# A GRU that feeds a ternary-weight FFN: load order, weight casts and step 0's products are rearranged at the start

## The chip, the cores and the metric

The kernel runs on one core of a Trainium2 chip. Its time is the device time of one execution in microseconds (us), as the median of several runs. The profile is of one further execution.

## What is computed

The input is x (128 sequences, 32 time steps, 256 features) with a start state cond (128 x 256). A GRU runs over the 32 steps, one after the other, since each step needs the state of the step before. Its states go through a feed-forward network with ternary weights, and x is added to the result.

```python
def cell(h, x):
    gi = x @ W_ih + b_ih
    gh = h @ W_hh + b_hh
    i_r, i_z, i_n = jnp.split(gi, 3, axis=-1)
    h_r, h_z, h_n = jnp.split(gh, 3, axis=-1)
    r = jax.nn.sigmoid(i_r + h_r)
    z = jax.nn.sigmoid(i_z + h_z)
    n = jnp.tanh(i_n + r * h_n)
    h_new = (1.0 - z) * n + z * h
    return (h_new, h_new)
...
wq_gu = ternary_quant(w_gate_up)          # groups of 64, scale = mean |w|
gate, up = jnp.split(jnp.einsum('bsd,hd->bsh', hs, wq_gu), 2, axis=-1)
h = jax.nn.silu(gate) * up
out = x + jnp.einsum('bsh,dh->bsd', rms_norm(h), ternary_quant(w_proj))
```

W_ih and W_hh are 256 x 768, w_gate_up is 2048 x 256, w_proj 256 x 1024.

## The kernel before, in words

**Layout.** The batch of 128 lies on the partitions. The 256 features are two halves of 128 (KD = 2, index k), so a product x @ W is two accumulating matmuls into PSUM. Every fp32 operand of a product is split into a high part (rounded to the matmul's fp32r type, `_hi`) and a low part (what the rounding left, `_lo`), and a product is three passes: hi x hi, hi x lo, lo x hi (`three_passes`, L672 to L680). So the GRU weights, raw in `wi` and `wh` (tiles of the program's `work` buffer, by which name the trace calls them), become `wi_hi`, `wi_lo`, `wh_hi`, `wh_lo`: ScalarE (ACT) casts the high part (L418, L427), VectorE (DVE) subtracts to get the low part (L586, L592). The state and the input are split in the same way (`xT_hi`, `xT_lo`; the start state goes to `grp_hi`, `grp_lo`).

**One GRU step t.** The bank `ps_rz` (512 columns) holds the sums for r and z, `ps_n` the two sums for n. ACT seeds both with the biases from a copy in SBUF, `bias` (L352 to L359). TensorE (PE) adds the input's products (`input_rz`, `input_n`) and the state's (`state_product`). ACT takes the sigmoid (`rz_gates`, L350), DVE forms r * h_n (`r_hn`, L498) and the sum `n_pre`, ACT the tanh, DVE the new state, PE transposes it, ACT and DVE split it for the next step.

**The order.** The order of each engine's work is written out by hand: each engine has a program of its own, runs it strictly in order, and waits on semaphores where it says so. Steps go in groups of GS = 4. The FFN on group g-1 runs between the GRU's parts of group g. In groups 0 and 1 (steps 0 to 7) the FFN weights are also made ternary, in 12 units of 128 x 512: ACT takes absolute value and sign (`q_abs`, `q_sign`, L396 and L401), PE sums groups of 64 (L795), ACT makes means (L408), GpSimd (POOL) and DVE form the quantized weights. The steady state is a loop over groups 2 to 6; group 7 and a last FFN stand behind it.

**The start, which the change touches.**

- SyncE's queue (SP) issues all loads in one order: both bias rows into `b_row`, the inputs of steps 0 and 1, W_ih in two halves, the transposed start state `cT`, W_hh in two halves, the start state `h_nat`, then the FFN weights and the rest of x (L237 to L251).
- ACT, in order: activation table, `xT_hi` of step 0, two casts of `wi_hi`, the two bias copies from PSUM (L420, L422), the start state's high part (L424), two casts of `wh_hi`, `xT_hi` of step 1, `q_abs` twice, `q_sign` twice. Then follows step 0's sigmoid.
- DVE, in order: sum of the bias rows (L581), `xT_lo` of step 0, two `wi_lo`, the start state's low part, two `wh_lo`, `xT_lo` of step 1. Then follows step 0's `r_hn`.
- PE, in order (L840 to L852): the biases are broadcast over the 128 partitions by matmuls of a row of ones with the bias rows in plain fp32, 256 + 256 columns into `ps_n` and 512 into `ps_rz`; four matmuls on an identity, `keep_clock(4)`; then the wait for both halves of `wi_lo`, step 0's input products, the wait for both halves of `wh_lo`, and step 0's state products.

Of the kernel before, what the change touches and what calls it, by code (L numbers as in the profile page):

```python
# [11 lines left out]
P = 128  # L31
KD = 2
GS = 4
# [3 lines left out]

# [17 lines left out]
def gru_ffn(nc, x, x_t, cond, cond_t, w_ih, w_hh, b_ih, b_hh, w_gate_up_t, w_proj_t, out):  # L57
# [7 lines left out]
    with ExitStack() as ctx:  # L65
# [78 lines left out]

# [7 lines left out]
        b_sum_ok, biased = sem("b_sum_ok"), sem("biased")  # L152
# [37 lines left out]

# [5 lines left out]

# [32 lines left out]
        def _(sp):  # L229
# [7 lines left out]
            for i, b in enumerate((b_ih, b_hh)):  # L237
                sp.dma_start(b_row[:, i, :], b.rearrange("(o n) -> o n", o=1)).then_inc(ld_b, 16)
            sp.dma_start(xT_all[:, :, 0:2, :], xt[:, :, 0:2, :]).then_inc(ld_x0, 16)
            for k in range(KD):  # L240
                sp.dma_start(wi[:, k], w_ih[k * P:(k + 1) * P, :]).then_inc(ld_wi[k], 16)
            sp.dma_start(cT[:], cond_t.rearrange("(k p) b -> p k b", p=P)).then_inc(ld_cT, 16)
            for k in range(KD):
                sp.dma_start(wh[:, k], w_hh[k * P:(k + 1) * P, :]).then_inc(ld_wh[k], 16)
            sp.dma_start(h_nat[:, 1, :], cond).then_inc(ld_c, 16)
# [38 lines left out]

# [62 lines left out]
        def _(act):  # L347
# [4 lines left out]
            def seed_rz(t):  # L352

                act.wait_ge(rz_ok, t)
                nc.scalar.copy(ps_rz[:], bias[:, 0, :]).then_inc(rz_seed, 1)
# [55 lines left out]

            act.wait_ge(consts, 2)
# [3 lines left out]
            for k in range(KD):  # L416
                act.wait_ge(ld_wi[k], 16)
                nc.scalar.copy(wi_hi[:, k], wi[:, k]).then_inc(wi_hi_ok, 1)  # L418
            act.wait_ge(biased, 1)
            nc.scalar.copy(bias[:, 1, :], ps_n[:]).then_inc(n_seed, 1)  # L420
            act.wait_ge(biased, 2)
            nc.scalar.copy(bias[:, 0, :], ps_rz[:]).then_inc(rz_seed, 1)  # L422
            act.wait_ge(ld_cT, 16)
            nc.scalar.copy(state("hi", GS - 1), cT[:]).then_inc(h_hi, 1)  # L424
            for k in range(KD):
                act.wait_ge(ld_wh[k], 16)
                nc.scalar.copy(wh_hi[:, k], wh[:, k]).then_inc(wh_hi_ok, 1)  # L427
            input_hi(1, 1)
# [65 lines left out]
        def _(dve):  # L494
# [88 lines left out]
            input_lo(0, 0)  # L583
# [87 lines left out]
        def _(pe):  # L671
# [10 lines left out]
            def input_rz(t, b):  # L682
                pe.wait_ge(rz_seed, t + 1)
                if isinstance(t, int) and 2 <= t < 2 + GS:
                    pe.wait_ge(x_lo_early, t - 1)
                else:
                    pe.wait_ge(x_lo, t + 1 if isinstance(t, int) and t < 2 else t + 1 - GS)
                three_passes(ps_rz[:], xT_hi[:, b], xT_lo[:, b], wi_hi, wi_lo, slice(0, 512), False)

            def input_n(t, b):  # L690
                pe.wait_ge(n_seed, t + 1)
                three_passes(ps_n[:, 0:D], xT_hi[:, b], xT_lo[:, b], wi_hi, wi_lo, slice(512, G3), False)

            def state_product(t, s):
# [11 lines left out]
                three_passes(ps_n[:, D:2 * D], hi, lo, wh_hi, wh_lo, slice(512, G3), True).then_inc(n_sum, 1)  # L706

# [105 lines left out]
            def iteration(g, ffn, carry):  # L813
                for s in range(GS):
                    t = GS * g + s
                    last = isinstance(g, int) and g == NG - 1
                    state_product(t, s)
# [21 lines left out]

            pe.wait_ge(consts, 6)  # L840
            pe.wait_ge(ld_b, 32)
            for i in range(2):
                mm = pe.matmul(ps_n[:, i * D:(i + 1) * D], ones_row[:], b_row[:, i, 2 * D:G3],
                               start=(i == 0), stop=(i == 1), skip_group_check=True)
# [47 lines left out]
```

## Time and profile before

| | before |
|---|---|
| median of 3 runs | 377.59 us (377.42 to 377.64) |
| profiled execution: span, first to last instruction | 376.7 us |
| what lies around the span, against the median of the runs | 0.9 us |
| busy: PE | 350.5 us (93%) |
| busy: DVE | 258.6 us (69%) |
| busy: ACT | 221.4 us (59%) |
| busy: POOL | 199.3 us (53%) |
| mean granted TensorE clock | 0.978 |

No device time of the profiled execution itself is given beside its span, so the 0.9 us compares that span with the median of the other runs. Busy shares average over the whole span; the start, the stretch with the quantization, and the loop have different limits and are read apart.

### The profile page before, as it was taken

To read this page: it belongs to the slowest core of one execution; us is meant where nothing else is said; L and a number is where in the kernel's file an instruction comes from. 1 tells how busy PE (TensorE), PEld (TensorE's weight loads), DVE (VectorE), ACT (ScalarE), POOL (GpSimd) and SP (SyncE) were. 2 spreads that over 40 slices of the span, in tenths; PEclk is the share of its full clock that TensorE was granted. 3 is DMA by queue.
4 is the path that set the end of the run, shared out by engine and by line. 5 is a ranking of instruction groups with operands and counts; after the bars stand their busy time and mean duration, and the time that the engine had idled before them with its cause. 6 is when DMAs were issued, how large, how long until landed. Compare 5 with 4: busy or idle time off the path is not lost.

```text
span 376.7 us, 5881 instructions
## 1 busy us (share of the span) xinstructions
PE 350.5 (93%) x1959; PEld 300.8 (80%) x1962; DVE 258.6 (69%) x484; ACT 221.4 (59%) x434; POOL 199.3 (53%) x165
## 2 busy tenths in 40 slices
PE   6957787788999999999999999999999999999995
PEld 3745566567888889888988888888988898888885
DVE  3499999997586566856585558656685658556644
ACT  5755576554746655666745574665566674547650
POOL 1067765585555536444625555553644472557882
PEclk9998888999999999999999999999999999999998
DMA  7980000370001000100010000100010001000101
GB/s 241 375 359 2 2 0 0 113 334 1 3 3 54 1 2 0 56 0 0 0 56 0 0 0 3 53 0 0 0 56 0 0 0 58 0 0 2 56 2 56
DMA packets 5394, 17.75 MB, mean 47 GB/s; under 512 B 386, under 2 KB 2050, under 8 KB 4996
## 3 DMA queue, kind: packets, MB, share of 16 engines
q1 hardware_dynamic: 5380, 17.57, 12.1%
q8 instruction: 8, 0.13, 0.2%
q14 instruction: 6, 0.05, 0.0%
HBM read 13.38 MB, written 4.19 MB: 47 GB/s over the span
## 4 chain that ended last, share of the span: by engine, by line
PE 75%; DVE 15%; issue 6%; DMA 1%; ACT 1%; SPq 0%; POOL 0%; DVEq 0%; POOLq 0%
PE ps_out L757 15%; PE ps_gate L718 14%; PE ps_up L718 13%; PE ps_rz L699 3%; PE ps_rz L700 3%; PE ps_rz L703 3%; PE ps_n L675 3%; PE ps_rz L675 3%; PE ps_n L676 3%; PE ps_n L678 3%; PE ps_rz L676 3%; PE ps_rz L678 3%; DVE q_sk L571 2%; DVE wguT L578 2%; PE ps_hT L711 2%
## 5 line engine op out<-in xcount | busy, mean ns | idle before, releaser
L311 POOL TENSOR_TENSOR hid_lo<-work,hid_hi 128x512 fp32r<-128x512 f32 x63 | 83.9, 1333 | 123.0 <-ACT hid_hi L378 123.0
L318 POOL TENSOR_TENSOR sq_sum<-sq_sum,work 128x512 f32<-128x512 f32 x54 | 70.8, 1310 | 0.0
L524 DVE TENSOR_TENSOR work<-work,ps_gate 128x512 f32<-128x512 f32 x64 | 43.8, 685 | 38.9 <-ACT work L374 38.1
L718 PE MATMUL ps_up<-grp_hi,wguT 128*128 128x512 f32 x118 | 47.4, 402 | 5.3 <-DVE work L534 5.3
L718 PE MATMUL ps_gate<-grp_hi,wguT 128*128 128x512 f32 x128 | 51.4, 401 | 0.0
L718 PE MATMUL ps_gate<-grp_lo,wguT 128*128 128x512 f32 x128 | 50.8, 397 | 0.0
L378 ACT CAST hid_hi<-work 128x512 fp32r<-128x512 f32 x63 | 38.8, 616 | 19.2 <-DVE work L534 19.2
L350 ACT ACTIVATE rz<-ps_rz 128x512 f32<-128x512 f32 x32 | 19.1, 596 | 50.8 <-PE ps_rz L703 50.8
L498 DVE TENSOR_TENSOR r_hn<-rz,ps_n 128x256 f32<-128x256 f32 x32 | 13.4, 419 | 48.7 <-PE ps_n L678 48.7
L534 DVE TENSOR_TENSOR work<-work,ps_up 128x512 f32<-128x512 f32 x59 | 40.5, 687 | 8.7 <-PE ps_up L718 7.2
L718 PE MATMUL ps_up<-grp_lo,wguT 128*128 128x512 f32 x118 | 46.4, 393 | 0.0
L374 ACT ACTIVATE work<-ps_gate 128x512 f32<-128x512 f32 x64 | 37.7, 589 | 11.0 <-PE ps_gate L718 11.0
L757 PEld LDWEIGHTS ps_out<-wpT,hid_hi 128*128 128x128 f32 x256 | 37.9, 189 | 4.3 <-DVE o_st L548 0.5
L757 PE MATMUL ps_out<-wpT,hid_hi 128*128 128x256 f32 x256 | 41.1, 283 | 0.1
L757 PE MATMUL ps_out<-wpT,hid_lo 128*128 128x256 f32 x256 | 41.0, 282 | 0.0
L757 PEld LDWEIGHTS ps_out<-wpT,hid_lo 128*128 128x128 f32 x256 | 35.1, 189 | 0.0
L388 ACT ACTIVATE work<-work 128x512 f32<-128x512 f32 x55 | 34.6, 629 | 0.0
L718 PEld LDWEIGHTS ps_up<-grp_hi,wguT 128*128 128x128 f32 x118 | 22.4, 189 | 11.4 <-DVE work L534 7.0
L294 POOL TENSOR_TENSOR o_st<-q_scale,q_abs 128x512 bf16<-128x512 bf16 x12 | 19.3, 1612 | 15.4 <-DVE q_scale L559 15.4
L675 PE MATMUL ps_rz<-wi_hi,xT_hi 128*128 128x512 f32 x64 | 26.2, 409 | 1.3 <-DVE wi_lo L586 0.8
L718 PEld LDWEIGHTS ps_gate<-grp_hi,wguT 128*128 128x128 f32 x128 | 24.4, 191 | 3.6
L718 PEld LDWEIGHTS ps_gate<-grp_lo,wguT 128*128 128x128 f32 x128 | 24.3, 190 | 3.4
(115 smaller groups left out, 772.1 us busy)
## 6 DMA issues: line engine op xcount, KB each, us to landing
x_all<-in_x_dram SPq DMA_DIRECT2D x1, 4096.0 KB, 12.2
out_dram<-o_st SPq DMA_DIRECT2D x7, 512.0 KB, 2.7
xT_all<-in_x_dram SPq DMA_DIRECT2D x1, 3072.0 KB, 19.5
x_all<-in_L_ffn_w_gate_up_dram SPq DMA_DIRECT2D x4, 512.0 KB, 9.2
x_all<-in_L_ffn_w_proj_dram SPq DMA_DIRECT2D x1, 1024.0 KB, 12.7
work<-in_L_cond_W_ih_dram SPq DMA_DIRECT2D x2, 384.0 KB, 4.2
work<-in_L_cond_W_hh_dram SPq DMA_DIRECT2D x2, 384.0 KB, 5.9
xT_all<-in_x_dram SPq DMA_DIRECT2D x1, 768.0 KB, 8.4
```

Source lines behind the costliest of these rows:

```text
L311: nc.gpsimd.tensor_tensor(hid_lo[:, j % RING], hid[:, j % 2], f32(hid_hi[:, j % RING]), ALU.subtract).then_inc(hid_lo_ok, 1)
L318: nc.gpsimd.tensor_tensor(sq_sum[:], sq_sum[:], hid_sq[:, j % 2], ALU.add).then_inc(sq_added, 1)
L374: nc.scalar.activation(sg[:, j % 2], ps_gate[:, j % 2], ACT.Sigmoid).then_inc(sg_ok, 1)
L378: nc.scalar.copy(hid_hi[:, j % RING], hid[:, j % 2]).then_inc(hid_hi_ok, 1)
L388: nc.scalar.activation(hid_sq[:, j % 2], hid[:, j % 2], ACT.Square).then_inc(hid_sq_ok, 1)
L524: nc.vector.tensor_tensor(gsg[:, j % 2], sg[:, j % 2], ps_gate[:, j % 2], ALU.mult).then_inc(gsg_ok, 1)
L534: nc.vector.tensor_tensor(hid[:, j % 2], gsg[:, j % 2], up_bank(G, j)[:], ALU.mult).then_inc(hid_ok, 1)
L675: pe.matmul(dst, hi[:, k, :], w_hi[:, k, cols], start=False, stop=False, skip_group_check=True)
L676: pe.matmul(dst, hi[:, k, :], w_lo[:, k, cols], start=False, stop=False, skip_group_check=True)
L678: mm = pe.matmul(dst, lo[:, k, :], w_hi[:, k, cols], start=False, stop=stop and k == KD - 1, skip_group_check=True)
L718: mm = pe.matmul(bank, w, part[:, k].rearrange("p s b -> p (s b)"), start=(k == 0 and i == 0), stop=(k == KD - 1 and i == 1))
L757: mm = pe.matmul(ps_out[:, s, :], part[:, j % RING, s * P:(s + 1) * P], wpT[:, j, :], start=(j == 0 and s % 2 == 0 and part is hid_hi), st ...
```

## The change

- SP's queue issues W_ih's two halves first, then W_hh's, then the FFN weights and x as before. The two bias rows, the inputs of steps 0 and 1, `cT` and `h_nat` are issued from ACT's program, ahead of its table load.
- DVE, not ACT, casts `wi_hi`; `xT_lo` of step 0 is put between the two casts.
- Step 0's input products are ordered by pass and by half k: hi x hi as each `wi_hi` comes, then lo x hi, then hi x lo as each `wi_lo` comes. Step 0's state products are ordered likewise (`first_input`, `first_state_product`).
- The biases for `ps_rz` and `ps_n` are no longer copied to SBUF before step 0's products are added to them. Instead PE makes the same bias sums once more, in the two banks of `ps_gate`, behind step 0's input products. ACT copies `bias` from there, behind its `wh_hi` casts.
- Nothing changes behind step 0, but for the semaphore counts of the seeds.

```diff
 # SyncE
-            for i, b in enumerate((b_ih, b_hh)):
-                sp.dma_start(b_row[:, i, :], b.rearrange("(o n) -> o n", o=1)).then_inc(ld_b, 16)
-            sp.dma_start(xT_all[:, :, 0:2, :], xt[:, :, 0:2, :]).then_inc(ld_x0, 16)
             for k in range(KD):
                 sp.dma_start(wi[:, k], w_ih[k * P:(k + 1) * P, :]).then_inc(ld_wi[k], 16)
-            sp.dma_start(cT[:], cond_t.rearrange("(k p) b -> p k b", p=P)).then_inc(ld_cT, 16)
             for k in range(KD):
                 sp.dma_start(wh[:, k], w_hh[k * P:(k + 1) * P, :]).then_inc(ld_wh[k], 16)
-            sp.dma_start(h_nat[:, 1, :], cond).then_inc(ld_c, 16)
 # ScalarE
+            for i, b in enumerate((b_ih, b_hh)):
+                act.dma_start(b_row[:, i, :], b.rearrange("(o n) -> o n", o=1)).then_inc(ld_b, 16)
+            act.dma_start(xT_all[:, :, 0:2, :],
+                          x_t.rearrange("(k p) t b -> p k t b", p=P)[:, :, 0:2, :]).then_inc(ld_x0, 16)
+            act.dma_start(cT[:], cond_t.rearrange("(k p) b -> p k b", p=P)).then_inc(ld_cT, 16)
+            act.dma_start(h_nat[:, 1, :], cond).then_inc(ld_c, 16)
             act.wait_ge(consts, 2)
             nc.scalar.activation(table[:], ones[:], ACT.Sigmoid)
             act.wait_ge(ld_x0, 16)
             input_hi(0, 0)
-            for k in range(KD):
-                act.wait_ge(ld_wi[k], 16)
-                nc.scalar.copy(wi_hi[:, k], wi[:, k]).then_inc(wi_hi_ok, 1)
-            act.wait_ge(biased, 1)
-            nc.scalar.copy(bias[:, 1, :], ps_n[:]).then_inc(n_seed, 1)
-            act.wait_ge(biased, 2)
-            nc.scalar.copy(bias[:, 0, :], ps_rz[:]).then_inc(rz_seed, 1)
             act.wait_ge(ld_cT, 16)
             nc.scalar.copy(state("hi", GS - 1), cT[:]).then_inc(h_hi, 1)
             for k in range(KD):
                 act.wait_ge(ld_wh[k], 16)
                 nc.scalar.copy(wh_hi[:, k], wh[:, k]).then_inc(wh_hi_ok, 1)
+            act.wait_ge(biased, 1)
+            for i in range(2):
+                nc.scalar.copy(bias[:, i, :], ps_gate[:, i, :]).then_inc(bias_ok, 1)
             input_hi(1, 1)
 # VectorE
-            input_lo(0, 0)
+            for k in range(KD):
+                dve.wait_ge(ld_wi[k], 16)
+                nc.vector.tensor_copy(wi_hi[:, k], wi[:, k]).then_inc(wi_hi_ok, 1)
+                if k == 0:
+                    input_lo(0, 0)
 # TensorE: step 0's state product
+            def first_state_product():
+                targets = ((ps_rz[:], slice(0, 512)), (ps_n[:, D:2 * D], slice(512, G3)))
+                hi, lo = state("hi", GS - 1), state("lo", GS - 1)
+                def product(part, w, k, dst, cols, stop=False):
+                    return pe.matmul(dst, part[:, k, :], w[:, k, cols], start=False, stop=stop,
+                                     skip_group_check=True)
+                pe.wait_ge(h_hi, 1)
+                for k in range(KD):
+                    pe.wait_ge(wh_hi_ok, k + 1)
+                    for dst, cols in targets:
+                        product(hi, wh_hi, k, dst, cols)
+                pe.wait_ge(h_lo, 1)
+                for k in range(KD):
+                    for dst, cols in targets:
+                        product(lo, wh_hi, k, dst, cols)
+                for (dst, cols), full in zip(targets, (rz_sum, n_sum)):
+                    for k in range(KD):
+                        pe.wait_ge(wh_ok, k + 1)
+                        mm = product(hi, wh_lo, k, dst, cols, k == KD - 1)
+                    mm.then_inc(full, 1)
 # TensorE: the start
-            for i in range(2):
-                mm = pe.matmul(ps_n[:, i * D:(i + 1) * D], ones_row[:], b_row[:, i, 2 * D:G3],
-                               start=(i == 0), stop=(i == 1), skip_group_check=True)
-            mm.then_inc(biased, 1)
-            pe.wait_ge(b_sum_ok, 1)
-            pe.matmul(ps_rz[:], ones_row[:], b_row[:, 0, 0:2 * D], start=True, stop=True).then_inc(biased, 1)
+            def biases(rz_bank, n_bank):
+                for i in range(2):
+                    pe.matmul(n_bank[:, i * D:(i + 1) * D], ones_row[:], b_row[:, i, 2 * D:G3],
+                              start=(i == 0), stop=(i == 1), skip_group_check=True)
+                pe.wait_ge(b_sum_ok, 1)
+                return pe.matmul(rz_bank, ones_row[:], b_row[:, 0, 0:2 * D], start=True, stop=True)
+            def first_input():
+                targets = ((ps_rz[:], slice(0, 512)), (ps_n[:, 0:D], slice(512, G3)))
+                def product(part, w, k):
+                    for dst, cols in targets:
+                        pe.matmul(dst, part[:, 0, k, :], w[:, k, cols], start=False, stop=False,
+                                  skip_group_check=True)
+                pe.wait_ge(x_hi, 1)
+                for k in range(KD):
+                    pe.wait_ge(wi_hi_ok, k + 1)
+                    product(xT_hi, wi_hi, k)
+                pe.wait_ge(x_lo, 1)
+                for k in range(KD):
+                    product(xT_lo, wi_hi, k)
+                for k in range(KD):
+                    pe.wait_ge(wi_ok, k + 1)
+                    product(xT_hi, wi_lo, k)
+            biases(ps_rz[:], ps_n[:])
             keep_clock(4)
-            pe.wait_ge(wi_ok, KD)
-            input_rz(0, 0)
-            input_n(0, 0)
-            pe.wait_ge(wh_ok, KD)
+            first_input()
+            biases(ps_gate[:, 0, :], ps_gate[:, 1, :]).then_inc(biased, 1)
             iteration(0, False, False)
```

Two places show how the rows of an engine's program move. First PE, between `keep_clock` and step 0's state product; `ps_gate` is the bank that the FFN's gate uses later. Before:

```order
L675 MATMUL ps_n<-wi_hi,xT_hi 128x256
L676 MATMUL ps_n<-wi_lo,xT_hi 128x256
L678 MATMUL ps_n<-wi_hi,xT_lo 128x256 x2
L699 MATMUL ps_rz<-wh_hi,grp_hi 128x512
L700 MATMUL ps_rz<-wh_lo,grp_hi 128x512
```

The end of the input products and the begin of the state products, in the program of the change:

```order
L858 MATMUL ps_rz<-wi_lo,xT_hi 128x512
L858 MATMUL ps_n<-wi_lo,xT_hi 128x256
L847 MATMUL ps_gate<-b_row,ones_row 128x256 x2
L850 MATMUL ps_gate<-b_row,ones_row 128x512
L691 MATMUL ps_rz<-wh_hi,grp_hi 128x512
L691 MATMUL ps_n<-wh_hi,grp_hi 128x256
```

The bias matmuls, which before stood only ahead of `keep_clock`, now stand a second time between the two products. The second place is ACT's program from the table load to step 0's sigmoid, before:

```order
L413 ACT_TABLE_LOAD
L413 ACTIVATE table<-ones 128x1
L370 CAST xT_hi<-xT_all 128x256
L418 CAST wi_hi<-work 128x768 x2
L420 COPY bias<-ps_n 128x512
L422 COPY bias<-ps_rz 128x512
L424 CAST grp_hi<-cT 128x2x128
L427 CAST wh_hi<-work 128x768 x2
```

And with the change, down to the sigmoid, its last row:

```order
L390 ACT_TABLE_LOAD
L390 ACTIVATE table<-ones 128x1
L341 CAST xT_hi<-xT_all 128x256
L394 CAST grp_hi<-cT 128x2x128
L397 CAST wh_hi<-work 128x768 x2
L400 COPY bias<-ps_gate 128x512 x2
L341 CAST xT_hi<-xT_all 128x256
L367 ACTIVATE q_abs<-x_all 128x512 x2
L372 ACTIVATE q_sign<-x_all 128x512 x2
L319 ACTIVATE rz<-ps_rz 128x512
```

The bias copies moved from ahead of the start state's cast to behind the `wh_hi` casts. Five instructions (the second `xT_hi`, two `q_abs`, two `q_sign`) stand between them and the sigmoid.

## Rows read from the trace of the kernel before

**Rows 1.** Windows: busy time of the engines, granted clock, DMA share, in three stretches

```profile
0.00:16.60 16.60, 13.05 (x40) 9.67 (x40) 5.61 (x8) 9.47 (x17) 1.40 (x12) 1.00 0.86 302
16.60:88.90 72.30, 54.12 (x247) 41.67 (x248) 70.50 (x110) 42.55 (x88) 47.61 (x35) 0.91 0.29 116
88.90:376.70 287.80, 283.30 (x1674) 249.47 (x1674) 182.47 (x367) 169.35 (x331) 150.27 (x118) 0.99 0.04 15
```

**Rows 2.** Chain that ended last: start us, length us, what; start and hand-over

```profile
2.38 4.99 DMA work<-in_L_cond_W_ih_dram
...
7.40 0.84 ACT wi_hi L418
...
9.30 0.77 PE ps_rz L675
...
15.19 0.60 PE ps_rz L703 x2
...
16.64 0.43 DVE r_hn L498
...
88.92 1.19 PE ps_up L718 x4
```

**Rows 3.** Timeline of PE: start us, us, instruction, tiles, count, idle before

```profile
2.79 2.04 PE L843 MATMUL ps_n<-b_row,ones_row 1*128 1x256 f32 x4 [2.79 <-DMA b_row<-in_L_cond_b_hh_dram]
4.62 1.91 PE L847 MATMUL ps_rz<-b_row,ones_row 1*128 1x512 f32 x2
6.46 2.08 PE L836 MATMUL ps_hT<-ident 128*128 128x128 f32 x8
```

**Rows 4.** Timeline of PE: input products cold, and step 1's warm

```profile
10.29 0.63 PE L675 MATMUL ps_rz<-wi_hi,xT_hi 128*128 128x512 f32 x1
...
10.72 0.63 PE L676 MATMUL ps_rz<-wi_lo,xT_hi 128*128 128x512 f32 x1
...
23.86 0.40 PE L676 MATMUL ps_rz<-wi_lo,xT_hi 128*128 128x512 f32 x1
...
24.10 0.40 PE L675 MATMUL ps_rz<-wi_hi,xT_hi 128*128 128x512 f32 x1
```

**Rows 5.** Timeline of ACT up to step 0's sigmoid (L350)

```profile
8.14 0.58 ACT L420 COPY bias<-ps_n 128x512 f32<-128x512 f32 x1
8.62 0.59 ACT L422 COPY bias<-ps_rz 128x512 f32<-128x512 f32 x1
9.09 0.42 ACT L424 CAST grp_hi<-cT 128x256 fp32r<-128x256 f32 x1
...
10.86 0.41 ACT L370 CAST xT_hi<-xT_all 128x256 fp32r<-128x256 f32 x1
12.02 1.15 ACT L396 ACTIVATE q_abs<-x_all 128x512 bf16<-128x512 f32 x2 [0.74 <-DMA x_all<-in_L_ffn_w_gate_up_dram]
13.07 1.13 ACT L401 ACTIVATE q_sign<-x_all 128x512 bf16<-128x512 f32 x2
15.83 0.60 ACT L350 ACTIVATE rz<-ps_rz 128x512 f32<-128x512 f32 x1 [1.62 <-PE ps_rz L703]
```

**Rows 6.** Windows, PE alone: busy, granted clock, DMA share, GB/s, around a rise

```profile
28.30:29.00 0.70, 0.69 (x6) 1.00 0.00 0
29.00:32.40 3.40, 3.40 (x11) 0.50 0.02 5
32.40:33.00 0.60, 0.60 (x7) 0.98 0.00 0
```

**Rows 7.** Timeline of DVE: the split of W_hh's two halves

```profile
10.27 1.83 DVE L592 TENSOR_TENSOR wh_lo<-work,wh_hi 128x768 fp32r<-128x768 f32 x2 [0.31 <-ACT wh_hi L427]
```

**Rows 8.** One line of DVE: ns min/median/max, a cast of 768 columns

```profile
L627 DVE CAST grp_lo<-new_lo x8: 551/551/1190, 49.9 to 342.8; 128x768 fp32r<-128x768 f32 x8
```

**Rows 9.** Timeline of SP's queue: issues of bias row and first input

```profile
1.14 0.23 SPq L238 DMA_DIRECT2D b_row<-in_L_cond_b_hh_dram  x1
...
1.42 0.42 SPq L239 DMA_DIRECT2D xT_all<-in_x_dram  x1
```

More of the change, by code:

```diff
@@ L151, in gru_ffn @@
         wi_hi_ok, wi_ok, wh_hi_ok, wh_ok = sem("wi_hi_ok"), sem("wi_ok"), sem("wh_hi_ok"), sem("wh_ok")
-        b_sum_ok, biased = sem("b_sum_ok"), sem("biased")
+        b_sum_ok, biased, bias_ok = sem("b_sum_ok"), sem("biased"), sem("bias_ok")
         q_sum = sem("q_sum")
@@ L354, in seed_rz @@
                 act.wait_ge(rz_ok, t)
+                if isinstance(t, int) and t == 1:
+                    act.wait_ge(bias_ok, 2)
                 nc.scalar.copy(ps_rz[:], bias[:, 0, :]).then_inc(rz_seed, 1)
@@ L682, in input_rz @@
             def input_rz(t, b):
-                pe.wait_ge(rz_seed, t + 1)
+                pe.wait_ge(rz_seed, t)
                 if isinstance(t, int) and 2 <= t < 2 + GS:
@@ L686, in input_rz @@
                 else:
-                    pe.wait_ge(x_lo, t + 1 if isinstance(t, int) and t < 2 else t + 1 - GS)
+                    pe.wait_ge(x_lo, 2 if isinstance(t, int) and t == 1 else t + 1 - GS)
                 three_passes(ps_rz[:], xT_hi[:, b], xT_lo[:, b], wi_hi, wi_lo, slice(0, 512), False)
             def input_n(t, b):
-                pe.wait_ge(n_seed, t + 1)
+                pe.wait_ge(n_seed, t)
                 three_passes(ps_n[:, 0:D], xT_hi[:, b], xT_lo[:, b], wi_hi, wi_lo, slice(512, G3), False)
@@ L816, in iteration @@
                     last = isinstance(g, int) and g == NG - 1
-                    state_product(t, s)
+                    if isinstance(g, int) and t == 0:
+                        first_state_product()
+                    else:
+                        state_product(t, s)
                     for u in summed(g, s):
```

## The prediction, made before the result was known

> **What bounds the kernel now.** I read the windows first, to see which engine is full in which stretch. In [rows 1] the first 16.6 us have no full engine; from 16.6 to 88.9 DVE works 70.5 of 72.3 us; from 88.9 on PE works 283.3 of 287.8 us. The chain of waits [rows 2] says the same: a load of W_ih until 7.4, its split, PE's products from 9.30, and from step 0's `r_hn` at 16.64 a chain of DVE instructions until PE takes over at 88.92. Between 16.64 and 88.92 the chain holds over 150 pieces and no DMA. The change touches nothing behind step 0, so all depends on one number: when `r_hn` of step 0 starts. I take every microsecond won or lost there as handed on to the end.
>
> **What is won: the wait for W_ih.** The loads of both halves of W_ih lose one 256 KB load and two bias rows ahead of them, and are issued some 1.1 us earlier. The second half landed at 7.4 [rows 2]; now it lands between 6.2 and 7.4. DVE casts instead of ACT: nearest rows are DVE's cast of the same size, 0.55 us at best [rows 8], and its subtraction, about 0.95 us each [rows 7]. At the worst `wi_hi` is ready at 7.4 + 0.95 = 8.4 and the second `wi_lo` at 8.4 + 1.9 = 10.3; at the best 8.7. Before, PE began at 9.30. Now PE's row has `keep_clock` until 6.46 + 2.08 = 8.5 [rows 3], so the input products start at 8.5, not earlier, whatever the loads do: 0.8 us won. They don't wait again: hi x hi and lo x hi take 4 x (0.43 + 0.21) = 2.6 us at the slow pace, so the last `wi_lo` is wanted at 11.7 and is there at 10.3. For the same reason the order by passes wins nothing more; the halves are all ready in time. The W_hh side has slack too: at worst `wh_lo` is ready at 10.3 + 0.4 + 1.9 = 12.6 and is wanted last of all.
>
> The granted DMA share is already 0.86 over the first 16.6 us [rows 1]. The Trainium skill (DMA: Bandwidth & Descriptors, Rules for kernel authors) says that spreading DMAs over two issuing engines does not help bandwidth and saves only issue time. By that rule the second queue gives only the later end of 6.2 to 7.4, and the trace's share agrees; the sum is the same at either end, since PE starts at 8.5.
>
> **What is paid on PE: the biases a second time.** The bias matmuls stand again between input and state products. The first set took from 2.79 to 6.46, 3.67 us [rows 3], at the slow pace. Which pace? A 512-column matmul took 0.43 us from start to start at 10.3 and 0.24 at 23.9 [rows 4], so PE was at 1.2 GHz and then at 2.4, though the clock column reads 1.00 in both. The input products are six of 512 and six of 256 columns: 6 x 0.43 + 6 x 0.21 = 3.84 us slow. If the clock rises at r, what is left runs in half the time, and input and second biases end at T = (r + 8.5 + 3.84 + 3.67) / 2 = (r + 16.0) / 2.
>
> When does it rise? Before, PE worked unbroken from 9.30 and was at the fast pace only at about 15.4 (the last pair of `ps_rz` took 0.60 instead of 0.86, [rows 2]), 6.1 us later. At 28.30 it resumed, and the granted clock was 0.50 until 32.4 and 0.98 after, 4.1 us after work resumed [rows 6]. Now there is no break between `keep_clock` and products: counted 4.1 us from the start of `keep_clock` (6.46) the rise is at 10.6, from the products' start (8.5) at 12.6, and with 6.1 us at 14.6. I take 12.0, near the products' case, because the biases and `keep_clock` ran from 2.79 to 8.5 and the clock had not risen by 9.3. T = 14.0. Ends: a rise at 8.5 gives T = 12.3, none gives 16.0.
>
> The Trainium skill (TensorE: Matmul & The Clock Gate, Part 1) says that the clock is throttled by default and that activity is looked at in free-running windows that don't restart with a kernel, so the point of the rise moves. By it T could lie anywhere between the ends above; the two delays here, 4.1 and 6.1 us, agree that it is not fixed.
>
> The bias rows come by ACT's queue now. Before, the second was issued at 1.14 and PE started at 2.79; the 256 KB load issued at 1.42 took until 4.45. So the biases start between 0 and 1.4 us later [rows 9, 3]. I take 0, since these are 3 KB rows, ahead in their queue. ACT's five issues cost it about 2 us, 0.23 to 0.43 each [rows 9], ahead of its table load; the load of x lands no earlier anyway, and ACT is idle later, so nothing.
>
> **What is paid on ACT: a queue behind the biases.** This decides. ACT runs in order, and the bias copies now wait for T. Behind them stand `xT_hi` of step 1, two `q_abs`, two `q_sign`, and only then step 0's sigmoid. Costs from [rows 5], start to start: the two copies 9.09 - 8.14 = 0.95; `xT_hi` 0.40; `q_abs` 13.07 - 12.02 = 1.05; `q_sign` 1.13. Together 3.5 us. Before, ACT had done all of it by 14.2 and sat idle 1.62 us until PE was ready at 15.83. Now the sigmoid starts at T + 3.5; with its 0.60 and 0.1 for the hand-over `r_hn` starts at T + 4.2. PE is not the later one: its state products take 3.84 us slow, 2.1 fast, and `rz_sum` comes before the last 0.4 us of them, so T + 3.4 at worst. The casts saved on ACT (2 x 0.83) are saved where ACT would now be idle: nothing. The q loads had landed by 12.02, before they are wanted.
>
> **The sum.** `r_hn` at 14.0 + 4.2 = 18.2 instead of 16.64: 1.6 us later. The profiled span of 376.7 becomes 378.3; the median of the runs is 0.9 us above that span, so 377.6 + 1.6 = **379.2 us**. Behind `r_hn` the order is unchanged and DVE has 1.8 idle us in 72 to take anything up.
>
> **Rivals.** About 0.2%, 0.76 us, is what a measurement can tell from no change.
> 1. *The clock stays down through the second biases.* A rise 6.1 us after 8.5 gives T = 15.3, none 16.0: `r_hn` at 19.5 to 20.2, loss 2.9 to 3.6, about 380.8. For it: the 6.1 us of before, and that the first biases, one row on the contracting side, did not raise the clock. Against it: the dense products now follow work without a gap.
> 2. *The clock rises at once*, at about 8.5 to 10.2. T = 12.3 to 13.1, `r_hn` at 16.5 to 17.3, time 377.5 to 378.3: no change that can be told. For it: the gap of 0.8 us ahead of the products is closed. Against it: 5.7 us of PE work before 8.5 raised nothing. A delay that is taken up between 16.6 and 88.9 would look the same.
> 3. *Faster: the start of PE itself is at the fast pace.* If the clock were up by about 6, `keep_clock` ends at 7.3 and the products wait only for the splits: the last `wi_lo` at 8.7 to 10.3 plus 0.35, biases 1.84, T = 11.0 to 12.4, `r_hn` at 15.2 to 16.6. The middle is 0.8 to 1.0 us earlier: 376.7. It decides for faster once T is under 16.64 - 0.76 - 4.2 = 11.7. Against it: the slow pace at 10.3.
> 4. *The overlap is empty*: the reordered passes do not do what they say, since all halves are ready at 8.5. That is part of the forecast; only with W_ih later than 9 would they count.
>
> **How the numbers follow.** The forecast's case (T from 13.3 to 14.8, so 378.5 to 380.0) gets 0.60, rival 1 0.18, rival 2 0.16, rival 3 0.06. The range takes in the forecast's case, rival 1 but for its extreme, and the upper part of rival 2: 378.0 to 381.0. Slower 0.78, same 0.16, faster 0.06.
>
> **What would show it.** In the profile after: the input products start at about 8.5 with no idle time before them; `ps_gate` matmuls of the biases follow at 12, ending at 14; ACT's copies of `bias` wait on PE, and its sigmoid L319 starts about 3.5 us behind them with no idle time before it, while PE had finished its state products; `r_hn` at about 18.2 waits for ACT, not PE; PE takes over at about 90.5 instead of 88.9. I am wrong if ACT idles before that sigmoid, if the copies come before 11.7, or if `r_hn` is late and the hand-over to PE at 88.9 is not.

## The result and the profile after

| | before | changed |
|---|---|---|
| median | 377.5 us (377.17 to 377.64, 4 runs) | 381.05 us (380.56 to 381.45, 4 runs) |
| ratio | | 1.0085, 95% interval 1.0067 to 1.0103 |
| profiled span | 376.7 us | 379.0 us |
| granted clock, mean | 0.978 | 0.973 |

The kernel became slower by 0.85%; between the medians lie 3.55 us. (The ratio is taken over the single runs; the two medians divided give 1.0094, inside the interval.) The forecast was 379.2 us (378.0 to 381.0) with 0.78 for slower. The sign is right; the median lies 0.05 us beyond the upper end of the range, and the loss is more than twice the 1.6 us that was forecast.

First the windows of the changed kernel, cut 2.3 us later than those of [rows 1], since the span grew by 2.3 us (us; busy of PE, PEld, DVE, ACT, POOL with counts; granted clock; DMA share; GB/s):

```profile
0.00:18.90 18.90, 13.24 (x47) 9.03 (x47) 6.95 (x12) 8.44 (x16) 1.39 (x12) 1.00 0.94 324
18.90:91.20 72.30, 53.33 (x249) 42.01 (x253) 70.53 (x110) 42.84 (x88) 48.05 (x36) 0.91 0.25 101
91.20:379.00 287.80, 283.48 (x1672) 249.70 (x1670) 181.49 (x365) 168.29 (x330) 149.94 (x118) 0.99 0.04 15
```

So moved, the two long stretches are as in [rows 1]: DVE works 70.5 of 72.3 us, PE 283.5 of 287.8. The start grew. Its chain of waits (start us, us, what):

```profile
17.09 0.52 ACT q_sign L372
17.61 0.49 ACT rz L319
...
18.19 0.43 DVE r_hn L471
...
90.28 1.19 PE ps_up L719 x4
```

Before, this chain came to `r_hn` at 16.64 by way of PE's products [rows 2]. Now it comes by ACT's `q_sign`, and `r_hn` starts at 18.19. PE takes over at 90.28 instead of 88.92. ACT's timeline shows why (start us, us, instruction, idle before it):

```profile
14.15 1.08 ACT L400 COPY bias<-ps_gate 128x512 f32<-128x512 f32 x2 [2.92 <-PE ps_gate L850]
...
15.11 0.42 ACT L341 CAST xT_hi<-xT_all 128x256 fp32r<-128x256 f32 x1
...
15.41 1.16 ACT L367 ACTIVATE q_abs<-x_all 128x512 bf16<-128x512 f32 x2
...
16.47 1.15 ACT L372 ACTIVATE q_sign<-x_all 128x512 bf16<-128x512 f32 x2
...
17.50 0.59 ACT L319 ACTIVATE rz<-ps_rz 128x512 f32<-128x512 f32 x1
```

The bias copies waited 2.92 us for PE, five instructions stood behind them, and the sigmoid began 3.35 us after the start of the copies, with no idle time ahead of it. In [rows 5] the same `q_abs` and `q_sign` were done by 14.2. PE's own timeline, the same columns:

```profile
3.86 2.04 PE L847 MATMUL ps_n<-b_row,ones_row 1*128 1x256 f32 x4 [3.86 <-DMA b_row<-in_L_cond_b_hh_dram]
...
7.54 2.08 PE L840 MATMUL ps_hT<-ident 128*128 128x128 f32 x8
...
9.27 0.77 PE L858 MATMUL ps_rz<-wi_hi,xT_hi 128*128 128x512 f32 x1
...
10.05 0.63 PE L858 MATMUL ps_rz<-wi_hi,xT_hi 128*128 128x512 f32 x1
...
10.99 0.40 PE L858 MATMUL ps_rz<-wi_hi,xT_lo 128*128 128x512 f32 x1
...
12.13 1.13 PE L847 MATMUL ps_gate<-b_row,ones_row 1*128 1x256 f32 x4
...
13.10 1.02 PE L850 MATMUL ps_gate<-b_row,ones_row 1*128 1x512 f32 x2
...
14.04 0.50 PE L691 MATMUL ps_rz<-wh_hi,grp_hi 128*128 128x512 f32 x1
...
15.19 0.40 PE L691 MATMUL ps_rz<-wh_hi,grp_lo 128*128 128x512 f32 x1
```

PE starts 1.07 us later than in [rows 3], for it waits for the bias row; the products start at 9.27, and 512-column matmuls pass from 0.63 to 0.40 us at about 10.6. The second biases end at 14.1. The state products behind them run at the fast pace here, with 0.40 us for 512 columns, and PE is done well before ACT.

Two more things differ. The first inputs land late. These are the issues and the wait:

```profile
1.28 0.22 ACTq L384 DMA_DIRECT2D b_row<-in_L_cond_b_hh_dram  x1
...
1.53 0.42 ACTq L385 DMA_DIRECT2D xT_all<-in_x_dram  x1
...
7.69 0.41 ACT L341 CAST xT_hi<-xT_all 128x256 fp32r<-128x256 f32 x1 [3.17 <-DMA xT_all<-in_x_dram]
...
8.48 0.55 DVE L558 CAST wi_hi<-work 128x768 fp32r<-128x768 f32 x1
8.94 1.82 DVE L563 TENSOR_TENSOR wi_lo<-work,wi_hi 128x768 fp32r<-128x768 f32 x2
```

The 256 KB of x landed 6.1 us after their issue, not 3.0, and DVE's second cast of W_ih stood behind `xT_lo`, which needs them. The last `wi_lo` was ready at 10.8, yet PE did not wait for it: it began at 9.27, straight behind `keep_clock`, with the passes that need `wi_hi` alone. And the last products of the kernel ran at half pace, here in the timeline and in a window of PE alone (busy, granted clock, DMA share, GB/s):

```profile
372.80 1.20 PE L758 MATMUL ps_out<-wpT,hid_hi 128*128 128x256 f32 x4
373.80 1.05 PE L758 MATMUL ps_out<-wpT,hid_lo 128*128 128x256 f32 x4
```

```profile
372.60:374.80 2.20, 2.20 (x10) 0.50 0.00 0
```

In the profile of before, the same last rows run at a granted clock of 1.00:

```profile
371.07 0.72 PE L757 MATMUL ps_out<-wpT,hid_hi 128*128 128x256 f32 x4
371.63 0.63 PE L757 MATMUL ps_out<-wpT,hid_lo 128*128 128x256 f32 x4
```

This is some 0.8 us that the start did not cause directly.

### The profile page after: what moved, and what is told of

Read it like the earlier page. It is cut to its first block, busy times and chain, and to the rows that moved or that the text cites. A ratio compares the mean times of both kernels' runs of the same rounds, so it can differ in the third digit from the quotient of the medians.

```text
span 379.0 us, 5888 instructions
## 1 busy us (share of the span) xinstructions
PE 350.1 (92%) x1965; PEld 300.7 (79%) x1968; DVE 259.0 (68%) x486; ACT 219.6 (58%) x432; POOL 199.4 (53%) x165
## 4 chain that ended last, share of the span: by engine, by line
PE 75%; DVE 15%; issue 5%; DVEq 0%; ACT 0%
PE ps_out L758 16%; PE ps_gate L719 14%; PE ps_up L719 13%; PE ps_rz L676 3%; PE ps_rz L680 3%; PE ps_rz L677 3%; PE ps_n L652 3%; PE ps_n L653 3%; PE ps_n L655 3%; PE ps_rz L653 3%; PE ps_rz L652 3%; PE ps_rz L655 3%; DVE q_sk L544 3%; DVE wguT L551 2%; PE ps_hT L712 2%
## 5 line engine op out<-in xcount | busy, mean ns | idle before, releaser
L345 ACT ACTIVATE work<-ps_gate 128x512 f32<-128x512 f32 x64 | 37.6, 588 | 12.1 <-PE ps_gate L719 12.1
L652 PE MATMUL ps_rz<-wi_hi,xT_hi 128*128 128x512 f32 x62 | 24.8, 400 | 2.0 <-ACT ps_rz L326 2.0
```

Of the source, the lines that this page charges most:

```text
L345: nc.scalar.activation(sg[:, j % 2], ps_gate[:, j % 2], ACT.Sigmoid).then_inc(sg_ok, 1)
L652: pe.matmul(dst, hi[:, k, :], w_hi[:, k, cols], start=False, stop=False, skip_group_check=True)
```

## The experiments

The theory is that of the forecast, the **queue theory**: the bias copies on ACT wait for PE's second biases, and the five instructions behind them hold up step 0's sigmoid. Its rivals: PE's products set it (**PE theory**, in a later form with the clock: **clock theory**), or the late loads do (**load theory**). Every ratio is to runs of the kernel before on the same chip. Kernels 1 to 4 ran on one chip, 5 to 8 on a second, 9 to 11 on a third, 12 on a fourth; medians of different groups are set side by side below, and the medians of the kernel before in these groups are 377.54, 377.46, 377.73 and 377.75 us.

**1. The copies out of the way.**

```diff
-            act.wait_ge(biased, 1)
-            for i in range(2):
-                nc.scalar.copy(bias[:, i, :], ps_gate[:, i, :]).then_inc(bias_ok, 1)
             input_hi(1, 1)
             q_abs_of(0)
             q_abs_of(1)
             q_signs(0)
             q_signs(1)
+            act.wait_ge(biased, 1)
+            for i in range(2):
+                nc.scalar.copy(bias[:, i, :], ps_gate[:, i, :]).then_inc(bias_ok, 1)
```

> The changed kernel, with ACT's two bias copies moved behind the two q_abs and two q_sign, so that only the copies wait for PE's second biases. Queue theory (the five ACT instructions behind the bias wait set step 0's sigmoid): ACT does them while it waited, the sigmoid starts with rz_sum at about 16.0 instead of 17.5, r_hn at about 16.8 instead of 18.19, and the time falls by 1.4 us against the change. PE theory (the second biases and the products behind them set it): r_hn stays at 18.2 and the time stays. Load theory (the late bias rows and first input set it): stays too.

Measured 380.93 us (378.69 to 381.39, 10 runs), ratio to before 1.0077 (1.0055 to 1.0098): no gain on the change. The queue theory missed. Its windows (columns as in the first fence) and timeline:

```profile
10.90:14.30 3.40, 3.40 (x15) 2.18 (x14) 1.49 (x3) 2.50 (x6) 0.00 (x0) 1.00 1.04 407
14.30:17.70 3.40, 3.40 (x11) 2.85 (x11) 0.00 (x0) 1.07 (x2) 0.00 (x0) 0.54 1.08 369
```

```profile
13.42 1.02 PE L850 MATMUL ps_gate<-b_row,ones_row 1*128 1x512 f32 x2
...
16.31 0.63 PE L691 MATMUL ps_rz<-wh_hi,grp_lo 128*128 128x512 f32 x1
...
18.04 0.60 ACT L319 ACTIVATE rz<-ps_rz 128x512 f32<-128x512 f32 x1 [2.50 <-PE ps_rz L691]
```

ACT idles 2.50 us now and PE is the late one. The granted clock fell to 0.54, the 1.2 GHz level, right behind the second biases, though PE had worked without a pause; the state products, down to the sum that the sigmoid needs, took 3.6 us instead of 2.1, and `r_hn` starts at 18.73. Eight of the ten runs lie from 380.5 to 381.4. Two were at 378.7 and 378.8, below even the 379.6 that was expected.

**2 to 4. The second biases and the loads, each undone, and both.** Without the second biases:

```diff
 # ScalarE, behind input_hi(0, 0)
+            act.wait_ge(biased, 1)
+            nc.scalar.copy(bias[:, 1, :], ps_n[:]).then_inc(bias_ok, 1)
+            nc.scalar.copy(bias[:, 0, :], ps_rz[:]).then_inc(bias_ok, 1)
...
-            act.wait_ge(biased, 1)
-            for i in range(2):
-                nc.scalar.copy(bias[:, i, :], ps_gate[:, i, :]).then_inc(bias_ok, 1)
 # TensorE
-            biases(ps_rz[:], ps_n[:])
+            biases(ps_rz[:], ps_n[:]).then_inc(biased, 1)
             keep_clock(4)
+            pe.wait_ge(bias_ok, 2)
             first_input()
-            biases(ps_gate[:, 0, :], ps_gate[:, 1, :]).then_inc(biased, 1)
```

> The changed kernel without PE's second biases: ACT copies the biases out of ps_n and ps_rz behind the first xT_hi, as before the change, and PE waits for the copies before step 0's products. Queue theory: nothing on ACT waits for a late PE result, q_abs starts as soon as its load is there (about 12 to 12.6), r_hn at about 15.5, 2.7 us earlier than the change and 1.1 earlier than before. Load theory: the products still start at 9.3 as the bias rows come late; r_hn no earlier than before, 16.6. If only the 1.8 us of PE work counts, r_hn at 16.4.

With the loads of before:

```diff
 # SyncE
+            for i, b in enumerate((b_ih, b_hh)):
+                sp.dma_start(b_row[:, i, :], b.rearrange("(o n) -> o n", o=1)).then_inc(ld_b, 16)
+            sp.dma_start(xT_all[:, :, 0:2, :], xt[:, :, 0:2, :]).then_inc(ld_x0, 16)
             for k in range(KD):
                 sp.dma_start(wi[:, k], w_ih[k * P:(k + 1) * P, :]).then_inc(ld_wi[k], 16)
+            sp.dma_start(cT[:], cond_t.rearrange("(k p) b -> p k b", p=P)).then_inc(ld_cT, 16)
             for k in range(KD):
                 sp.dma_start(wh[:, k], w_hh[k * P:(k + 1) * P, :]).then_inc(ld_wh[k], 16)
+            sp.dma_start(h_nat[:, 1, :], cond).then_inc(ld_c, 16)
 # ScalarE
-            for i, b in enumerate((b_ih, b_hh)):
-                act.dma_start(b_row[:, i, :], b.rearrange("(o n) -> o n", o=1)).then_inc(ld_b, 16)
...
-            act.dma_start(h_nat[:, 1, :], cond).then_inc(ld_c, 16)
```

> The changed kernel with all loads on SP's queue in the order of before, all else as changed. Bias rows land at 2.8 instead of 3.9, so PE's start, the second biases and the queue behind them all come 1.1 us earlier: r_hn at about 17.1 if the clock rises as early, and the time falls by about 1 us. If the load order of the change is worth anything, the first products wait for wi_hi and r_hn does not move. A late clock rise would hide up to 1.5 us of it.

And with both edits together:

> Loads as before and no second biases; what is left of the change is DVE's cast of W_ih and the products by pass. PE's products start at about 8.5 without a gap, the queue on ACT is free of PE: q_abs at 12.0 when its load lands, sigmoid at 14.3, r_hn at about 15.0, 1.6 us earlier than before: 375.9 us, faster than both kernels. If the q loads landing at 12.0 do not bound it but PE does with a late clock rise, r_hn at 16 and 377. Clock theory of the tail: any run can be 0.8 us longer where the clock falls in the last products, whatever the start does.

| median us | with second biases | without |
|---|---|---|
| loads of the change | 381.05 (the change) | 377.97 (377.14 to 379.43) |
| loads of before | 379.98 (379.56 to 380.16) | 376.73 (376.38 to 377.42) |

The ratios to before are 1.0018 (1.0001 to 1.0035) for the second kernel, 1.0056 (1.0036 to 1.0077) for the third, 0.9976 (0.9962 to 0.999) for the fourth. The second biases cost 3.1 us with the one set of loads and 3.25 with the other; the load order costs 1.1 and 1.2. From the ratios instead of the medians it is 2.5 and 3.0 us, and 1.1 and 1.6. Both are harmful alone and they add up. In the profile of the second kernel `r_hn` is at 15.21, near the 15.5 of the queue theory; that its products still start late, at 9.15, is the share of the loads. From the timeline of the fourth kernel:

```profile
8.06 0.77 PE L857 MATMUL ps_rz<-wi_hi,xT_hi 128*128 128x512 f32 x1
...
14.09 0.60 ACT L324 ACTIVATE rz<-ps_rz 128x512 f32<-128x512 f32 x1
...
14.78 0.42 DVE L470 TENSOR_TENSOR r_hn<-rz,ps_n 128x256 f32<-128x256 f32 x1 [2.71 <-ACT rz L324]
```

PE starts its products straight behind `keep_clock`, and `r_hn` is at 14.78; 15.0 was expected. The gain expected, 1.6 us, was counted from 16.64 and came out as 0.8 (see 8). For the third kernel about 380 was expected, with `r_hn` at 17.1. The time came as expected, `r_hn` did not: in the third kernel the profile fell on a late clock rise: the products start 1.2 us earlier than with the loads of the change, but `r_hn` did not move.

```profile
8.09 0.77 PE L857 MATMUL ps_rz<-wi_hi,xT_hi 128*128 128x512 f32 x1
...
11.44 0.63 PE L857 MATMUL ps_rz<-wi_lo,xT_hi 128*128 128x512 f32 x1
...
18.29 0.42 DVE L470 TENSOR_TENSOR r_hn<-rz,ps_n 128x256 f32<-128x256 f32 x1 [2.21 <-ACT rz L324]
```

The last input products still take 0.63 here, 0.40 in the profile of the change. Seven runs, not one profile, carry the 1.1 us; the slowest of them, 380.16, lies below the fastest of the change, 380.56. Here too the clock fell behind the second biases, at about 15.7, while PE was busy.

**5 and 6. One row or 128.** The second biases contract over one row, that is, only one of the 128 partitions holds values for them. Here they contract over all 128, a matrix of ones with the bias row and 127 rows of zeros, once on the change and once on kernel 1:

```diff
+            nc.gpsimd.memset(b_wide, 0.0).then_inc(wide_ok, 1)
+            pool.wait_ge(wide_ok, 1)
+            nc.gpsimd.memset(ones_wide, 1.0).then_inc(wide_ok, 1)
 # VectorE, behind the sum of the bias rows
+            nc.vector.tensor_copy(b_wide[0:1], b_row[:]).then_inc(wide_row, 1)
 # TensorE, in place of the second biases()
+            pe.wait_ge(wide_ok, 2)
+            pe.wait_ge(wide_row, 1)
+            for i in range(2):
+                pe.matmul(ps_gate[:, 1, i * D:(i + 1) * D], ones_wide, b_wide[:, i, 2 * D:G3],
+                          start=(i == 0), stop=(i == 1), skip_group_check=True)
+            pe.matmul(ps_gate[:, 0, :], ones_wide, b_wide[:, 0, 0:2 * D],
+                      start=True, stop=True).then_inc(biased, 1)
```

`b_wide` is 128 x 1536, `ones_wide` 128 x 128.

> The changed kernel, whose second bias matmuls contract over all 128 rows (a matrix of ones with the bias row and 127 rows of zeros) instead of one; columns and results are the same. Clock theory (the granted clock falls behind the one-row matmuls, and step 0's state products then run at 1.2 GHz): the clock stays at 2.4 GHz through the state products; ACT's queue still sets r_hn at 18.2, so the time falls only by what the slow products had added in the median, to about 380. If the rows make no difference to the clock, no change from 381.0.

> e1_copies_late with the 128-row second biases. Clock theory: neither ACT's queue nor slow products stand in the way; the sigmoid starts at about 16.1, r_hn at 16.8, all runs near the two lowest of e1 (378.7), 2.2 us under e1's median of 380.9. Queue theory alone (clock no part of it): as e1, 380.9. It tells why moving the copies alone gave nothing.

The fifth measured 380.97 (380.52 to 381.26), as the change; its fall of 1 us was not seen. In its profile the clock rises late, at about 12.8, the state products run at 0.40 us for 512 columns, and the sigmoid still waits for ACT's queue, until 18.38. The sixth measured 379.42 (378.76 to 380.86), ratio to before 1.0056 (1.0037 to 1.0075), 1.5 us under kernel 1, with seven of nine runs between 378.8 and 379.7. None of the changed kernel's eight runs (four in the result, four in 12) is under 380.5. The interval of the ratio does overlap that of kernel 1, 1.0055 to 1.0098, whose runs also fall in two groups; it is the count of runs in the lower group, seven of nine against two of ten, that tells them apart. Its timeline:

```profile
13.95 1.02 PE L891 MATMUL ps_gate<-x_all 128*128 128x512 f32 x2
...
15.86 0.39 PE L702 MATMUL ps_rz<-wh_hi,grp_lo 128*128 128x512 f32 x1
...
17.55 0.42 DVE L479 TENSOR_TENSOR r_hn<-rz,ps_n 128x256 f32<-128x256 f32 x1 [5.00 <-ACT rz L327]
```

Behind full-row biases the state products run at 0.39 us. `r_hn` comes 0.75 us later than the 16.8 expected, since the clock rose at about 12.6 and the biases ended at 15.0. So two hindrances stand side by side behind T, the end of the second biases: ACT's queue (3.35 us) and the slowed state products (3.6 us in kernel 1). Taking away one (kernel 1 or kernel 5) gains nothing, since the other takes its place; taking away both (kernel 6) gains 1.5 us. The second hindrance is not in every execution: in the change's first profile the state products took 2.1 us. The expectation of kernel 5 overlooked that slow products can still end within ACT's queue, as they do in kernel 12.

**7. The cast alone.** The kernel before with DVE casting `wi_hi`, `xT_lo` between the two casts, nothing else.

```diff
 # VectorE
-            input_lo(0, 0)
+            for k in range(KD):
+                dve.wait_ge(ld_wi[k], 16)
+                nc.vector.tensor_copy(wi_hi[:, k], wi[:, k]).then_inc(wi_hi_ok, 1)
+                if k == 0:
+                    input_lo(0, 0)
```

> The kernel before, with DVE casting W_ih instead of ACT, nothing else. ACT is then free for the bias copies by 7.5; wi_lo comes 0.1 to 0.3 us earlier than before, as the second half lands at 7.1 to 7.4 and 0.55 + 1.8 us follow. If the cast is what e4 gained by, 376.7; if the products by pass are (they let PE start at 8.1 instead of 9.3), 377.3 or no change.

Measured 378.08 (377.49 to 379.23, 12 runs), ratio 1.0024 (1.001 to 1.0037): slightly slower, which neither theory had. DVE and PE:

```profile
7.08 0.56 DVE L582 CAST wi_hi<-work 128x768 fp32r<-128x768 f32 x1 [0.91 <-DMA work<-in_L_cond_W_ih_dram]
7.56 1.82 DVE L587 TENSOR_TENSOR wi_lo<-work,wi_hi 128x768 fp32r<-128x768 f32 x2
```

```profile
9.43 0.80 PE L676 MATMUL ps_rz<-wi_hi,xT_hi 128*128 128x512 f32 x1 [1.11 <-DVE wi_lo L587]
```

The cast is shorter (0.56 for 0.83), but both subtractions now stand behind the second cast on one engine, where the first used to run while the second half was still on its way. The last `wi_lo` comes at 9.4, no earlier. Why the median is 0.6 us up is open; `r_hn` is at 15.57 in this profile, but the profiled execution, 377.5 us, is one of the two fastest of the twelve.

**8. Before, once more**, without an edit.

> The kernel before, once more, for a second profile of it. If the profile shown of before caught a late clock rise (its span of 376.7 lies 1.0 above the 375.7 that most executions have), this one rises earlier, at about 12 to 13, with r_hn at about 15.5; if not, r_hn is at 16.6 again and the difference lies elsewhere.

377.49 us, span 375.7. PE and DVE:

```profile
12.39 0.34 PE L675 MATMUL ps_n<-wi_hi,xT_hi 128*128 128x256 f32 x1
```

```profile
15.56 0.42 DVE L498 TENSOR_TENSOR r_hn<-rz,ps_n 128x256 f32<-128x256 f32 x1 [2.74 <-PE ps_n L678]
```

The clock rose at 12.4, not 15.4, and `r_hn` is at 15.56. Of the 28 runs beside kernels 1 to 4, the spans lie from 374.2 to 377.1 with the median at 375.7. The profile that the forecast was made on was therefore a late one, by 1.0 us, and what lies around the span is 1.8 us, not 0.9.

**9. The order by passes alone.** Kernel 4 with the casts of W_ih back on ACT:

```diff
 # ScalarE, ahead of the bias copies
+            for k in range(KD):
+                act.wait_ge(ld_wi[k], 16)
+                nc.scalar.copy(wi_hi[:, k], wi[:, k]).then_inc(wi_hi_ok, 1)
 # VectorE
-            for k in range(KD):
-                dve.wait_ge(ld_wi[k], 16)
-                nc.vector.tensor_copy(wi_hi[:, k], wi[:, k]).then_inc(wi_hi_ok, 1)
-                if k == 0:
-                    input_lo(0, 0)
+            input_lo(0, 0)
```

> The kernel before with step 0's products by pass and nothing else changed (ACT casts W_ih, loads on SP, no second biases). The bias copies then end at 9.1 on ACT and PE's products wait for them, so PE starts at 9.1 to 9.3 instead of 9.3 to 9.7 and no pass is ahead of its half: no change from before, 377.4. If the order by passes alone is what e4 gained by, 376.7.

377.94 (376.74 to 378.52), ratio 0.9999 (0.9983 to 1.0016): no change. PE waited for ACT's bias copies until 8.8. Cast and order pay only together: kernels 7 and 9 gain nothing, kernel 4 has both and gains 0.8 us. The profiles suggest why: with the cast on DVE but the old order, PE waits for the last `wi_lo` until 9.43; with the new order but the cast on ACT, it waits for ACT's copies until 8.8; with both it begins at 8.06.

**10 and 11. Better than both.** First `q_sign` behind the sigmoid:

```diff
             q_abs_of(1)
-            q_signs(0)
-            q_signs(1)
 # in step 0, behind q_abs_of(2) and q_abs_of(3)
+                    if isinstance(g, int) and g == 0 and s == 0:
+                        q_signs(0)
+                        q_signs(1)
```

> e4_both_back with the two q_sign moved from ahead of step 0's sigmoid to behind step 1's q_abs. In e4's profile the sigmoid started at 14.09 with q_sign ending there and rz_sum at 14.05, so both set it: if ACT's queue is the later one in most executions, up to 0.8 us less than e4 (376.7), 376.0; if PE is, no change.

376.30 (375.87 to 376.77, 12 runs), ratio 0.9957 (0.9943 to 0.997). The sigmoid starts at 12.97 there:

```profile
12.97 0.60 ACT L324 ACTIVATE rz<-ps_rz 128x512 f32<-128x512 f32 x1
13.66 0.42 DVE L471 TENSOR_TENSOR r_hn<-rz,ps_n 128x256 f32<-128x256 f32 x1 [1.72 <-ACT rz L324]
```

This version is faster than both kernels, by 1.4 us against the one before. Then, on top, full-row work on PE from the start, with the first biases made as in kernel 5 and `keep_clock(4)` cut to one:

```diff
 # TensorE, in place of the waits for consts and ld_b
+            pe.wait_ge(wide_ok, 1)
+            for _ in range(6):
+                pe.matmul(ps_hT[:, 0, :], ones_wide, ones_wide, start=True, stop=True)
+            pe.wait_ge(wide_ok, 2)
+            pe.wait_ge(wide_row, 1)
 # in biases()
-                    pe.matmul(n_bank[:, i * D:(i + 1) * D], ones_row[:], b_row[:, i, 2 * D:G3],
+                    pe.matmul(n_bank[:, i * D:(i + 1) * D], ones_wide, b_wide[:, i, 2 * D:G3],
...
-            keep_clock(4)
+            keep_clock(1)
```

> e9 with PE kept busy from 1.1 us on: six matmuls on a matrix of ones until the bias row is there, then the first biases with 128 rows. Clock theory: with full-row work from the start the clock rises by 8, the input products take 1.9 us instead of 3.8, and only the load of the FFN weights (11.9) and two q_abs hold the sigmoid: r_hn at about 13.8, 375.6. If rows make no difference to the clock, the rise stays at 10.6 to 12.4 and the time is e9's or 0.3 worse, since the bias sums end 1.5 us later.

375.63 (374.8 to 378.17, 12 runs), ratio 0.9944 (0.9925 to 0.9962). The median is lower, but the interval overlaps that of kernel 10, and two of twelve runs are at 378. The profile fell on one of these:

```profile
9.44 0.80 PE L871 MATMUL ps_rz<-wi_hi,xT_hi 128*128 128x512 f32 x1 [0.74 <-ACT bias L402]
...
12.81 0.62 PE L871 MATMUL ps_rz<-wi_lo,xT_hi 128*128 128x512 f32 x1
...
16.16 0.42 DVE L479 TENSOR_TENSOR r_hn<-rz,ps_n 128x256 f32<-128x256 f32 x1 [3.54 <-ACT rz L332]
```

Here full-row work from 1.0 us on, with gaps of 0.6 us ahead of the biases and 0.7 us ahead of the input products, had not raised the clock by 12.8, so the expectation did not hold in this execution. The products also start 1.3 us later than in kernel 10 (9.44 for 8.18), behind ACT's bias copies. Whether the clock rose early in the other executions is not shown.

**12. The change, once more**, without an edit.

> The changed kernel once more, for a second profile of it and more times. Theory: r_hn is at T + 4.1, with T (end of the second biases) between 14.0 and 15.0 by when the clock rises, and the last down product either at 2.4 GHz or, as in the first profile, at 1.2 (0.8 us more). If both vary from execution to execution, this one has a span of 287.8 + 72.1 + r_hn, 0.8 more if the tail is slow; if the slow tail belongs to the change itself, it is slow again.

380.84 (380.57 to 381.35), span 378.8. PE alone in a window, then DVE:

```profile
15.00:18.00 3.00, 3.00 (x12) 0.60 1.09 357
```

```profile
18.89 0.42 DVE L471 TENSOR_TENSOR r_hn<-rz,ps_n 128x256 f32<-128x256 f32 x1 [2.21 <-ACT rz L319]
```

The clock rose 1.5 us later than in the first profile, `r_hn` came 0.7 later, and the last products ran at full pace (0.72 and 0.63 us). `r_hn` and the span are what was expected for an execution with a fast tail. So the slow tail is no fixed part of the change; it is also in the profiles of kernels 1, 9 and 10 and in part in that of kernel 2, and in neither of the two of before. The granted clock fell to a mean of 0.60 in the state products here, from 15.6 on, and `r_hn` still waited for ACT.

## Why the prediction was right, and where it was not

**All hangs on `r_hn` of step 0: right.** From `r_hn` to PE's taking over it is 72.3 us before, 72.1 after, 72.3 in the second profile of before, and 72.1 to 72.2 in kernels 1 to 4. From there to the end it is 287.8, or up to 0.9 more where the last products are slow.

**ACT's queue: right, and not alone.** The sum had T + 4.2; it was 14.1 + 4.1 = 18.2, forecast 18.2. Kernels 1, 5 and 6 show that the state products, at the lower clock behind the one-row biases, would have held `r_hn` up as long wherever the clock falls there: `r_hn` at T + 4.3 in kernel 1. The forecast had 3.4 us for them at worst against 3.5 on ACT, so the tie was in its numbers, but it drew from it only that ACT is later.

**T: right by luck, by errors that cancel.** The bias rows were taken at 0 late (bounds 0 to 1.4); they came 1.07 late. The clock rise was taken at 12.0 and came at 10.6. The two balanced, and T was 14.1 for 14.0. In the second profile the rise came at 12.1, as forecast, and T was 14.8. That the products start at 8.5 failed: 9.27, since `keep_clock` moved with the biases. The 8.5 was misread besides: the 2.08 us of the four matmuls in [rows 3] hold the drain of the last, and the next matmul starts 1.73 us after the first of them (7.54 to 9.27), so without the late bias rows it is 8.2, or 8.06 as in kernel 4.

**The loads.** That the inputs on ACT's queue land no earlier, and that this costs nothing, was half right: they landed 3.2 us later, and it cost nothing, as PE began behind `keep_clock` with no idle time. The landing of W_ih was forecast for 6.2 to 7.4 and came at about 5.0, 2.4 us earlier than before. It won nothing, for the reason given, and the second cast had to wait for x in any case. The undone load order gives 1.1 to 1.2 us, which fits the delay of the bias row. The Trainium skill (DMA: Bandwidth & Descriptors, Rules for kernel authors) says that a second issuing engine does not add bandwidth; the trace agrees: the DMA share was near full, 0.94 over the start, and what W_ih gained (2.4 us), x lost (3.2 us). The forecast drew too much from it: it was the order of the loads, not the number of queues, that brought W_ih forward.

**The size: too small.** The step that failed is the base of the sum, the 16.64 from which the delay was counted. The profile of before had `r_hn` at 16.64, an execution with the median span at 15.56 (kernel 8): 1.1 us. The forecast also took the rest of the program to be unmoved; a slow tail (0.8 us, first profile) or a later rise (0.7 us, second) came on top. 1.6 + 1.1 + 0.7 to 0.8 = 3.4 to 3.5 us, near the 3.55 between the medians. How often each of the last two comes is not shown, so they are sizes seen in one profile each, not means. A 0.9 us gap between span and median was read as what lies around the span; it was 1.8, so the profiled execution of before took about 378.5 us, more than any of the four runs beside it.

**The rivals.** A clock that stays down through the second biases did not happen in either profile; what came in three of four profiles with one-row second biases was its neighbour, a clock that falls behind them. The time landed at rival 1's figure, 380.8, without its cause: T was 14.1 and 14.8, not 15.3 to 16.0. *The overlap is empty* was wrong as a statement on this kernel. The order of before waits for both halves of `wi_lo`, which were ready at 10.8 here and at 8.7 to 10.3 in the forecast's own figures; the forecast's start at 8.5 needed the new order. It is empty only with the casts on ACT (kernel 9).

## What to carry to other kernels

A wait moved into an in-order queue costs what stands behind it: before a copy that nobody needs soon is put ahead of work that a chain needs, count both. Where two hindrances end within about half a microsecond of each other, an experiment that removes one shows nothing; remove both, and then each. A single profile of a program whose start depends on the clock's rise can be a microsecond off its median, so compare its span with the spans of several executions before a sum is hung on it.

## What the hardware showed that was not expected

- Behind 1.9 us of matmuls that contract over a single row, with PE busy without a pause, the granted clock fell from 1.00 to 0.50 in three of four profiles: 0.1 us behind them in kernel 1 (mean 0.54 over the next 3.4 us), 0.8 us in kernel 12, 1.5 us in kernel 3. In the change's first profile it stayed at 1.00. With the same columns over 128 rows it stayed at 1.00 in both profiles while the state products ran, and they took 0.39 to 0.40 us per 512 columns (kernels 5 and 6). That the rows are the cause rests on these six profiles and on the counts of runs in kernels 1 and 6.
- The rise at the start came at very different times. The Trainium skill (TensorE: Matmul & The Clock Gate, Part 1) says that the gate follows PE's activity in windows that run freely; the traces agree that the rise is not tied to the start: with PE work from 2.7 or 2.8 us on it came at 15.4 in one profile of the kernel before and at 12.4 in the other.
- With the weights first on SP's queue and the small loads on ACT's, the 3 KB bias rows could be used 1.07 us later and a 256 KB load landed 3.2 us later, with the DMA share at 0.94; in kernel 1 the same load was in use 1.8 us later than before (6.21 for 4.45), so this delay varies.
